# The first layer's selective scans on tiles of 4 states x 32 channels, in a two-layer kernel on one core

## What is computed

```python
h = silu(depthwise_conv(in_proj(x)))                    # 384 channels
xs = stack([rows, columns, rows[::-1], columns[::-1]])  # K = 4 directions
x_dbl = einsum('bkdl,kcd->bkcl', xs, x_proj_weight)     # dts (rank 12), Bs, Cs (16 rows each)
delta = softplus(einsum('bkrl,kdr->bkdl', dts_r, dt_projs_weight) + bias)
def step(hstate, inp):                                  # along l = 0 .. 4095
    hstate = exp(dl[..., None] * A) * hstate + (dl * ul)[..., None] * bl[:, :, None, :]
    y = einsum('bkdn,bkn->bkd', hstate, cl)             # sum over the 16 states
ys = ys + Ds * u
y = ys[:, 0] + ys[:, 2, :, ::-1] + transposed(ys[:, 1] + ys[:, 3, :, ::-1])
# layer norm over channels, out_proj
```

## Time and profile before

| | |
|---|---|
| time, median of 3 runs | 27913.34 us (27886.87 to 27956.28) |
| profiled execution, its own time | 27921.66 us |
| its span | 27919.9 us, 261599 instructions |
| busy over the span | PE 89%, PEld 38%, DVE 91%, ACT 64%, POOL 84% |
| mean granted TensorE clock | 0.975 |
| costliest group | the scans with s_dbu, L1049 on DVE: 14960.7 us, x12236, mean 1269 ns |

### The profile page before, as it was taken

How to read it: one execution, slowest core, us unless ns; L and a number is a source line. 1 busy time by engine, 2 the same in 40 slices (tenths; PEclk the granted TensorE clock), 3 DMA queues, 4 the chain that set the end, 5 groups by cost and what they waited for, 6 DMA issues and landing times. The chain is left out here.

```text
span 27919.9 us, 261599 instructions
## 1 busy us (share of the span) xinstructions
PE 24874.1 (89%) x70946; PEld 10612.0 (38%) x70946; DVE 25291.2 (91%) x22482; ACT 17866.2 (64%) x30091; POOL 23560.1 (84%) x10168
## 2 busy tenths in 40 slices
PE   8788988998888899889888888988889988888888
PEld 3333443443443344344344434434334433333332
DVE  8899999999999999999999999999851189999996
ACT  2477777777777777777777777777423266666662
POOL 1599999999999999999999999999502189999994
PEclk9999999999999999999999999999999999999999
DMA  5533333333333343333333333333543277777778
GB/s 202 193 140 148 150 140 145 147 142 141 151 143 142 145 152 138 145 150 144 140 149 149 138 147 149 141 143 150 178 133 109 79 232 230 229 229 230 230 230 293
DMA packets 1194275, 4583.10 MB, mean 164 GB/s; under 512 B 254368, under 2 KB 292272, under 8 KB 827472
## 3 DMA queue, kind: packets, MB, share of 16 engines
q1 hardware_dynamic: 1093568, 4217.15, 42.5%
q10 hardware_dynamic: 99248, 349.22, 3.4%
HBM read 3907.28 MB, written 658.64 MB: 164 GB/s over the span
## 5 line engine op out<-in xcount | busy, mean ns | idle before, releaser
L1049 DVE TENSOR_TENSOR_SCAN s_h<-s_dA,s_state,s_dbu 128x512 f32<-128x512 f32 x12236 | 14960.7, 1269 | 59.2 <-ACT s_dA L884 50.7
L971 POOL TENSOR_TENSOR s_dbu<-s_du,s_b_sb 128x1536 f32<-128x1536 f32 (+1 forms) x4610 | 14188.6, 3084 | 430.9 <-DMA s_b_sb<-rows 428.7
L884 ACT ACTIVATE s_dA<-s_delta,s_negA 128x512 f32<-128x512 f32 x12288 | 8289.9, 685 | 5515.3 <-DVE s_h L1049 5501.6
L711 PE MATMUL s_y_ps<-s_hc,s_ident 128*128 128x512 f32 x17920 | 8785.2, 602 | 1.5 <-DVE s_hc L1059 1.5
L983 POOL TENSOR_TENSOR s_hc_pool<-s_h,s_c_sb 128x512 f32<-128x512 f32 (+1 forms) x4864 | 7843.8, 1617 | 575.4 <-DVE s_h L1049 514.6
L721 PE MATMUL s_y_ps<-s_hc_pool,s_ident 128*128 128x512 f32 x12800 | 6379.7, 600 | 105.2 <-ACT s_yo L846 105.2
L1059 DVE TENSOR_TENSOR s_hc<-s_h,s_c_ps 128x1024 f32<-128x1024 f32 (+1 forms) x5632 | 5526.0, 981 | 169.5 <-issue 140.9
L711 PEld LDWEIGHTS s_y_ps<-s_hc,s_ident 128*128 128x128 f32 x17920 | 3491.1, 195 | 2162.5 <-issue 1932.4
L1049 DVE TENSOR_TENSOR_SCAN s_h<-s_dA_sb,s_state,s_dA 128x512 f32<-128x512 f32 x3060 | 3816.0, 1266 | 295.1 <-PE s_dA L672 290.8
L701 PE MATMUL s_c_ps<-s_bc,s_sel 96*128 96x512 bf16 x6400 | 2369.0, 390 | 1455.2 <-DVE s_hc L1059 1441.2
L721 PEld LDWEIGHTS s_y_ps<-s_hc_pool,s_ident 128*128 128x128 f32 x12800 | 2379.7, 193 | 2786.9 <-issue 2532.9
(11 more groups left out here) (175 smaller groups left out, 17734.1 us busy)
## 6 DMA issues: line engine op xcount, KB each, us to landing
s_b_sb<-rows SPq DMA_DIRECT2D x1794, 1024.0 KB, 6.8
s_c_sb<-rows SPq DMA_DIRECT2D x1216, 1024.0 KB, 5.2
s_u<-U SPq DMA_DIRECT2D x257, 768.0 KB
Y<-s_yo ACTq DMA_DIRECT2D x256, 768.0 KB, 3.8
s_prev<-Y SPq DMA_DIRECT2D x128, 768.0 KB, 4.4
s_u<-U SPq DMA_DIRECT2D x193, 256.0 KB
U<-f_row SPq DMA_DIRECT2D x24, 2048.0 KB, 17.3
U<-f_col SPq DMA_DIRECT2D x24, 2048.0 KB, 7.1
```

Of the source, the lines that this page charges most:

```text
L711: last = pe.matmul(y_ps[:, t, :], ident[:, :], hc[:, s % 2, j, :], start=begins(g, s), stop=nd > 1 and s == NS - 1)
L884: act.activation(place, delta[g % 2][:, t, :], ACT.Exp, scale=negA[g % 2][:, a:a + 1]).then_inc(dA_ready, 1)
L971: pool.tensor_tensor(dbu[:, i % AHEAD, :, :], a, b, ALU.mult).then_inc(dbu_ready, 1)
L1049: dve.tensor_tensor_scan(h[:, s % (2 * GROUP), j, :], decay, given, initial, ALU.mult, ALU.add).then_inc(scanned, 1)
```

## The change

The first layer's call of `scan_phase` is replaced by a new function `packed_scans`. The units, the 48 scans of 128 x 512 in each and all other stages stay. What differs:

- **Tiles.** A tile holds 4 states x 32 channels: partition 32r+c is state r of its group and channel c of its block of 32. A unit has 12 steps (4 groups of states x 3 blocks of 128 channels) of 4 tiles.
- **Inputs of the scans.** All 48 are made on data that lie position by channel, and transposed by PE into PSUM (`turn_input`). ACT scales 10 of the 16 states (`BY_ACT`), in 40 instructions of 128 x 384; POOL scales 6 (`BY_POOL`), in 6 instructions of 128 x 48 x 32 with B as a broadcast.
- **Decays.** ACT reads a copy of delta that is spread over the 4 states by DMA: delta is stored to `delta_dram` once per unit and read back by 12 DMAs (`spread_delta`). It writes to SBUF, 7 tiles ahead.
- **Products with C.** In each step DVE takes tile 0 (C spread by PE in PSUM, one fp32 matmul per group with 32 rows of weights in place of 16 bf16 ones per unit), POOL tiles 1 to 3 in one instruction of 128 x 1536 (C spread by 4 DMAs).
- **Sums.** `fold`, 128 x 32, adds the 4 states of a tile: 4 matmuls of 32 columns of weights, each to its own 32 partitions of `y_ps`.
- **State.** POOL copies the last column of h (`tensor_copy`, 128 x 4) in 7 units of 8; before, ACT saved it with a factor `keep`.
- `rest`, and the weights loaded for each unit, go away.

```diff
+    DECAYS, INPUTS, H_RING, REP = 7, 3, 3, 4
+    BY_ACT = ((0, 1), (0, 1, 2), (0, 1, 2), (0, 1))
+    BY_POOL = ((2, 3), (3,), (3,), (2, 3))
+    on_pe = dict(dt=(0, 1, 2), turn_du=(6, 7, 8), xproj=(9, 9, 10), rows=11, c=(2, 5, 8, 11))
+    on_act = dict(rows=0, dt=(1, 2, 3), soft=3, turn_du=(7, 8, 9), take=11, evacuate=(0, 1, 2), store=3)
+    on_pool = dict(du=5)
+    SCALE_ACT = {0: (1, 0), 1: (1, 1), 3: (2, 0), 4: (2, 1), 6: (3, 0), 7: (3, 1), 9: (4, 0), 10: (4, 1)}
+    SCALE_POOL = {0: (1, 0), 3: (2, 0), 6: (3, 0), 7: (3, 1), 9: (4, 0), 10: (4, 1)}
...
+            def spread_delta(g, j):
+                x = NJ * g + j
+                if x >= REP:
+                    before, last = divmod(x - REP, NJ)
+                    eng.wait_ge(dA_ready, before * TILES + (STEPS - NJ + last + 1) * NI)
+                for r in range(R):
+                    eng.dma_start(delta_rep[32 * r:32 * r + 32, x % REP, :, :],
+                                  delta_dram[g % 2, :, j, :].rearrange("(i c) t -> c i t", c=32)).then_inc(rep_in[x % REP], 16)
...
+            def turn_input(n, i):
+                tile, x = n * NI + i, n // NJ
+                if n % NJ == 0 and i == 0:
+                    pe.wait_ge(scaled_act, QB * scaled_to(BY_ACT, x + 1))
+                    pe.wait_ge(scaled_pool, scaled_to(BY_POOL, x + 1))
+                wait(pe, scanned, tile - INPUTS + 1)
+                for b in range(QB):
+                    last = pe.transpose(x_ps[:, tile % INPUTS, b * 128:(b + 1) * 128],
+                                        scaled[:, x % 2, b, n % NJ * NI + i, :, :].rearrange("p r c -> p (r c)"), ident[:, :])
+                last.then_inc(input_turned, 1)
...
+            def state_sum(n):
+                g, m = divmod(n, STEPS)
+                if m < NJ:
+                    direct(g, m)
+                pe.wait_ge(hc_ready, n + 1)
+                pe.wait_ge(own_ready, own_to(n + 1))
+                for i in range(NI):
+                    last = pe.matmul(y_ps[32 * i:32 * i + 32, m % NJ, :], fold[:, :], hc[:, n % 2, i, :],
+                                     start=m < NJ and not opens(g) and not folds(g), stop=m >= STEPS - NJ)
+                last.then_inc(summed, 1)
...
+                for b in range(part * QB // 2, (part + 1) * QB // 2):
+                    for r in BY_ACT[x % NG]:
+                        s = x % NG * R + r
+                        act.activation(scaled[:, x % 2, b, :, r, :], duT[g % 2][:, b, :, :], ACT.Copy,
+                                       scale=rowsT[g % 2][:, b, s:s + 1]).then_inc(scaled_act, 1)
...
+                wait(act, scanned, tile - DECAYS + 1)
+                a = m * NI + i
+                act.activation(dA[:, tile % DECAYS, :], delta_rep[:, x % REP, i, :], ACT.Exp,
+                               scale=negA[:, direction(g), a:a + 1]).then_inc(dA_ready, 1)
...
+            def take_du(g):
+                pool.wait_ge(delta_ready, g + 1)
+                pool.wait_ge(delta_stored, 16 * (g + 1))
+                pool.wait_ge(loaded[g % 2], 32 * (g // 2 + 1))
+                pool.tensor_tensor(delta[:, :, :], delta[:, :, :], u[g % 2][:, :, :], ALU.mult).then_inc(du_ready, 1)
...
+                pool.tensor_tensor(scaled[:, x % 2, :, :, r, :], duT[g % 2][:, :, :, :],
+                                   rowsT[g % 2][:, :, s:s + 1].unsqueeze(3).broadcast_to([128, QB, NJ * NI, 32]),
+                                   ALU.mult).then_inc(scaled_pool, 1)
...
+                pool.wait_ge(scanned, (n + 1) * NI)
+                if goes_on(g):
+                    pool.tensor_copy(state[:, m * NI:(m + 1) * NI], h[:, n % H_RING, :, T - 1]).then_inc(state_saved, 1)
+                if m == 0:
+                    pool.wait_ge(c_in[g % 2], 16 * R * (g // 2 + 1))
+                wait(pool, summed, n - 1)
+                first = own(m)
+                c = c_sb[g % 2][:, m // NJ:m // NJ + 1, :].broadcast_to([128, NI - first, T])
+                pool.tensor_tensor(hc[:, n % 2, first:NI, :], h[:, n % H_RING, first:NI, :], c, ALU.mult).then_inc(hc_ready, 1)
...
+                if i == 0:
+                    wait(dve, hc_ready, n - H_RING + 1)
+                dve.wait_ge(dA_ready, tile + 1)
+                dve.wait_ge(input_turned, tile + 1)
+                dve.tensor_tensor_scan(h[:, n % H_RING, i, :], dA[:, tile % DECAYS, :], x_ps[:, tile % INPUTS, :],
+                                       initial, ALU.mult, ALU.add).then_inc(scanned, 1)
...
+                dve.tensor_tensor(hc[:, n % 2, 0, :], h[:, n % H_RING, 0, :], c_ps[:, :], ALU.mult).then_inc(own_ready, 1)
...
-    scan_phase(nc, "s0", (B, K0, ND0, 1, R0), U0, Y0, rows0, arg["a_xproj"], arg["a_dt"], arg["a_small"],
-               arg["a_D"], arg["keep"], arg["ident"], arg["select"])
+    packed_scans(nc, U0, Y0, rows0, scratch("delta0", (2, 128, ND0, T)), arg["a_xproj"], arg["a_dt"], arg["a_bias"],
+                 arg["a_logs"], arg["a_D"], arg["ident"], arg["fold"], arg["pick"])
```

More of the change, by code:

```diff
@@ L1981 @@
     ident = np.eye(128, dtype=f)
+    fold = np.tile(np.eye(32, dtype=f), (4, 1))
+    pick = np.zeros((2 * N_STATE, 4, 4, 32), f)
+    for n in range(N_STATE):
+        pick[N_STATE + n, n // 4, n % 4] = 1
     select = np.zeros((XROWS, 2 * N_STATE, 128), f)
@@ L1999 @@
         "x": a["x"].reshape(B, CH, L),
-        "ident": ident, "select": select[:, N_STATE:].reshape(XROWS, -1), "keep": keep, "group_mean": group_mean,
+        "ident": ident, "fold": fold, "pick": pick.reshape(2 * N_STATE, 4, 128), "select": select[:, N_STATE:].reshape(XROWS, -1), "keep": keep, "group_mean": group_mean,
         "mean_384": np.full((128, 128), 1 / D0, f), "mean_64": mean_64, "mean_192": mean_192,
@@ L2004 @@
         "a_conv_b": columns(la["conv_b"], ND0),
-        "a_xproj": xproj(la["x_proj_weight"], R0, ND0),
+        "a_xproj": np.concatenate([la["x_proj_weight"][:, R0:], la["x_proj_weight"][:, :R0]], 1)
+                     .reshape(K0, 2 * N_STATE + R0, ND0, 128).transpose(3, 0, 2, 1),
         "a_dt": la["dt_projs_weight"].reshape(K0, ND0, 128, R0).transpose(0, 3, 1, 2),
-        "a_small": small(la["dt_projs_bias"], la["A_logs"], ND0),
+        "a_bias": la["dt_projs_bias"].reshape(K0, ND0, 128).transpose(2, 0, 1),
+        "a_logs": la["A_logs"].reshape(K0, ND0, 4, 32, 4, 4).transpose(5, 3, 0, 4, 1, 2).reshape(128, K0, -1),
         "a_D": la["Ds"].reshape(K0, ND0, 128).transpose(2, 0, 1),
```

379 lines of the change are left out of this document (added).

## The result

The changed kernel takes 26,336 us in the median of its four runs (26,306 at best), beside 27,926 for the kernel before, run in turn with it on the same chip (27,887 to 27,956). The ratio is 0.9428, with an interval of 0.9409 to 0.9446: 5.7% faster. The forecast was 26,520, so it missed by 0.7%, and the time lies inside the range. One of the four runs after took 34,141 us at a mean granted clock of 0.695; the ratio leaves it out, and the median of the other three is 26,321. The profiled execution took 26,350.9 us.

The account below looks back on a forecast made before the run. DVE was taken to set the pace: 63.6 us of work plus 4.6 of waits make 68.2 us a unit, 5.45 less than 73.65; times 256, 1395 us off 27,913 gives 26,520 us, range 26,050 to 27,550.

Parts of the forecast that it names:

- The bound before: Kernel before: DVE sets the pace with 71.2 us of a 73.65 us unit, POOL 1 us behind at 70.3.
- DVE's sum after: DVE per unit: 48 scans, 56.6 us, and 12 products of 512 elements at 0.58, together 63.6 us against 71.2.
- New waits: DVE's scans waiting for inputs transposed by PE: 1.1 us for 12 tiles before, so 4.6 us a unit for 48.
- POOL's scaling: POOL's six input instructions per unit, with B as a broadcast: 3.40 us each, 20.4 us in place of 40.8.
- rival A: GpSimd dearer or inputs later, still faster: unit 70 to 73.4 us; at 71.5, 27,360 us; chance 0.17.
- POOL's 12 products: POOL's products with C: 12 instructions of 1536 elements at 3.40 us, 40.8 us a unit in place of 26.1.
- the copy: POOL's copy of the state, 128 x 4, in 7 of 8 units: 0.2 us each, 2.1 us a unit.
- costs at most some tenths: ACT, 60.3 us a unit, runs up to 7 tiles ahead of DVE; its longest stretch without a decay is 7.8 us.
- Rival B: PE's four narrow sums run one by one: PE needs 74.2 us a unit, 28,670 us, slower; chance 0.05.
- PE's work itself: PE's work per unit: transposes 21.1 us, sums 10.6 to 21.1, the rest 10.5 and 1.3; sum 43.5 to 54.
- Rival C: TensorE's clock stays at the lower level: PE needs at least 87 us a unit, 31,330 us, slower; chance 0.04.
- The signs: Named as showing it right: stage about 17,450 us, POOL 95% or more, DVE about 93%, sums starting together, scaling 3.4 us.

Follow-up runs that it names:

- Run 12: Changed kernel with GpSimd's scaling reading 1536 separate elements of the spread C in place of the broadcast B: 27,101 us, ratio 0.9714.
- Runs 3 and 4: Changed kernel, with some of ACT's scalings a step earlier (26,101 us), or with softplus replaced by an exponential without its two table loads (25,992 us).
- run 7: Changed kernel with each tile's four transposes done twice into the same place: 27,859 us, ratio 0.9989.
- run 1: Changed kernel with PE's four narrow sums of step n-2 put ahead of the first transposes for step n+1: 25,722 us, ratio 0.9216.

## Why the prediction was right, and where only by luck

- **The bound before, and DVE's sum after, hold.** 63.6 us of work from the earlier trace rows against 67.44 - 4.2 = 63.2 measured; 4.6 us of waits against 4.2. The unit is 0.76 us below the forecast, 195 us, which is the miss.
- **The mechanism of those waits was wrong.** The step that failed is "New waits": they were priced as scans that wait for transposed inputs, 1.1 us for 12 tiles scaled to 48, with an idle of 1000 to 1500 us to be seen there. It is 47 us. The idle is real (930 us) and stands before DVE's product. The sentence on which it turns is in the same step: the same sums wait for POOL's product, "but the ring of h (3 steps) holds DVE by the same product anyway". The tighter ring is `hc`, of two steps, and DVE writes it too. Where PE's order, that ring and the ring of inputs close a loop of 4.9 us beside a step of 5.3, it needed an addition of its own.
- **POOL's scaling was mis-sized**, 3.40 for 2.70, and six of them are 4.2 us: POOL's work is 62.1 us, not 66.7. The step took the value from the earlier trace rows, "with no reason for a gain"; those rows show only two full operands.
- **These two errors cancel.** Run 12 is the kernel as the prediction saw it, with 66.3 us on POOL. Its unit is 70.39, not 68.2, and its time 27,101. So 4.6 us of waits was too little for that load, where 7.1 were due, and it came out right because the load was lighter. 27,101 is in the range, but it is rival A's ground, not the forecast's.
- **POOL's 12 products, the copy, the decays, the scans** came as written, the copy at 0.15 for 0.2.
- **ACT "costs at most some tenths"** failed. It has about the 60.3 us of work that were summed (59.6 from start to start), and its longest stretch without a decay did fit; decays hold DVE for 43 us in all, nearly all of it once, at the start. But its scalings are late for PE, which the sum didn't look at. Runs 3 and 4 take 0.9 and 1.3 us a unit away by easing it.
- **Rival B was rightly doubted and wrongly priced.** The narrow sums run four side by side. Had they not, it would have cost 32,535, not 28,670: the price was PE's work, where the loop decides. PE's work itself, put at 43.5 to 54 us, is an estimated 48.8.
- **Rival C** happened in a small way: 0.95 granted in the stage, in gaps behind waits, as the prediction said. That transposes keep the clock up, read there from one place, run 7 shows over the whole stage.
- **The signs.** Stage (17,264 us for some 17,450), DVE's share and the start of the sums came as named. POOL at 95% or more, its scaling at 3.4 us and DVE's idle at PE's transposes did not. That rings, not an engine, set the pace was to show in POOL and DVE both below 93%. POOL is at 92%, DVE at 94%, so the sign came only by half; yet run 1 gains 614 us by order alone.

## What to carry to other kernels

Add up not only each engine's work but each loop that a ring closes: from the release of a slot through every instruction queued ahead of its refill, to the wait for it, and hold that against the time that the fullest engine takes for the same step. In an engine's own order put what others already wait for ahead of what has still to wait itself; here it was worth 2.3%. When a forecast comes true, undo its assumptions one at a time: here two wrong terms made one right sum.

## What the runs showed of the hardware

- GpSimd's fp32 product of 1536 elements takes 3.40 us from start to start on two different full tensors, and 2.70 us if one operand has only 4 separate elements per partition or is the same memory as the other. Layout of the destination makes no difference (3.40 in runs of 32).
- Four fp32 matmuls with 32 columns of weights into four quarters of the partitions run fully side by side: 0.47 us from the first record's start to the last one's, 0.99 until the next instruction, beside 3.44 for four of 128 columns. Entering and leaving that form costs 0.09 us each.
- With transposes doubled, TensorE's granted clock was 1.00 over the stage; with single ones, and the gaps between them, 0.95.
